# Attention in a decoder layer: the order of normalising, rope and query parts in a batch's third and fourth step

## The reference, cut to what matters

```
q = rope((ln(x) @ Wq.T).reshape(B, L, 32, 64));  k = rope((ln(x) @ Wk.T).reshape(B, L, 8, 64))
v = (ln(x) @ Wv.T).reshape(B, L, 8, 64)
attn = einsum(q, k) * 64**-0.5, causal;  p = softmax(attn);  out = einsum(p, v)
x = x + out.reshape(B, L, 2048) @ Wo.T
```

## Time and profile before

| | |
|---|---|
| median of 3 runs | 1603.34 us (1602.89 to 1606.78) |
| the profiled execution's own time | 1601.83 us |
| its span, first to last instruction | 1600.1 us |
| busy in the span: PE, DVE, ACT, POOL | 93%, 86%, 67%, 56% |

### The profile page before, as it was taken

How to read it: one execution, slowest core, us unless ns; L and a number is a source line. 1 busy time by engine, 2 the same in 40 slices (tenths; PEclk the granted TensorE clock), 3 DMA queues, 4 the chain that set the end, 5 groups by cost and what they waited for, 6 DMA issues and landing times. The chain is left out here.

```text
span 1600.1 us, 28647 instructions
## 1 busy us (share of the span) xinstructions
PE 1488.9 (93%) x8952; PEld 1306.1 (82%) x8952; DVE 1377.6 (86%) x3583; ACT 1066.6 (67%) x2464; POOL 902.1 (56%) x1024
## 2 busy tenths in 40 slices
PE   6799999999999999999999999779879999999998
PEld 4678878878878888888888887658779999999997
DVE  7799888989989898898898989668768889988996
ACT  3578778778777778778777777533146666666664
POOL 7668658667666666767667666268413443334432
PEclk9899999999999999999999999976589999999999
DMA  4000000000000000000000000042348788777761
GB/s 179 1 14 21 1 14 21 1 14 21 1 14 20 1 14 21 1 14 2 20 14 1 1 1 1 1 141 102 131 137 233 223 230 236 223 209 210 201 185 45
DMA packets 61925, 116.87 MB, mean 73 GB/s; under 512 B 22718, under 2 KB 22846, under 8 KB 61776
## 3 DMA queue, kind: packets, MB, share of 16 engines
q1 hardware_dynamic: 51328, 98.05, 19.0%
q0 software_dynamic: 10304, 16.94, 5.3%
q10 hardware_dynamic: 144, 0.07, 0.0%
HBM read 101.89 MB, written 20.51 MB: 76 GB/s over the span
## 5 line engine op out<-in xcount | busy, mean ns | idle before, releaser
L567 POOL TENSOR_SCALAR probs<-probs,row_inv 128x512 f32<-128x512 f32 (+3 forms) x512 | 296.2, 598 | 55.5 <-DVE row_inv L446 55.5
L330 ACT ACTIVATE probs<-probs,neg_max 128x512 f32<-128x512 f32 (+3 forms) x512 | 281.8, 552 | 12.2 <-DVE neg_max L439 6.7
L558 POOL TENSOR_TENSOR rot<-rot,sin 128x512 f32<-128x512 f32 (+1 forms) x96 | 124.3, 1295 | 251.2 <-DVE rot L458 248.7
L427 DVE TENSOR_TENSOR pt_lo<-bank,pt_hi 128x512 fp32r<-128x512 f32 (+1 forms) x384 | 217.8, 595 | 43.5 <-ACT pt_hi L323 43.5
L1285 POOL DMA_INDIRECT out<-ctx_raw,idx x46 | 93.8, 2038 | 266.4 <-ACT ctx_raw L1440 215.5
L439 DVE CUSTOM_DVE_ANT_0 probs<-bank,causal 128x512 f32<-128x512 f32 (+3 forms) x512 | 228.0, 481 | 7.3 <-PE bank L211 5.3
L223 PE MATMUL bank<-ident,probs 128*128 128x128 f32 x1280 | 184.1, 274 | 43.6 <-DVE pt_lo L427 43.2
L223 PEld LDWEIGHTS bank<-ident,probs 128*128 128x128 f32 x1280 | 150.8, 140 | 84.4 <-DVE pt_lo L427 51.7
L323 ACT ACTIVATE pt_hi<-bank 128x512 fp32r<-128x512 f32 (+1 forms) x384 | 186.5, 519 | 49.0 <-PE bank L223 43.6
L1367 PE MATMUL bank<-xt_hi,gu_hi 128*128 128x256 f32 x736 | 208.5, 283 | 3.5 <-issue 1.9
L1367 PE MATMUL bank<-xt_hi,gu_lo 128*128 128x256 f32 x736 | 206.6, 281 | 0.0
(11 more groups left out here) (204 smaller groups left out, 3980.6 us busy)
## 6 DMA issues: line engine op xcount, KB each, us to landing
gu_raw<-in_gate_up SPq DMA_DIRECT2D x92, 512.0 KB, 3.9
dn_raw<-in_down SPq DMA_DIRECT2D x92, 256.0 KB, 3.8
w_raw<-in_wqkv SPq DMA_DIRECT2D x8, 768.0 KB, 4.4
w_raw<-in_wo_rows SPq DMA_DIRECT2D x8, 512.0 KB, 3.5
h_rows<-ln_h SPq DMA_DIRECT2D x16, 256.0 KB, 2.1
out<-x_res SPq DMA_DIRECT2D x4, 1024.0 KB, 4.5
x_res<-in_x SPq DMA_DIRECT2D x3, 1024.0 KB, 11.2
ctx_raw<-in_ctx SPq DMA_DIRECT2D x2, 512.0 KB, 6.8
```

The source lines that it names most:

```text
L330: nc.scalar.activation(row, row, ACT.Exp, bias=neg_max[:, hb, i:i + 1], scale=-1.0, accum_out=row_sum[:, hb, i:i + 1]).then_inc(s["exp_don ...
L427: nc.vector.tensor_tensor(dst, src, hi.bitcast(F32), ALU.subtract).then_inc(sem_, 1)
L558: nc.gpsimd.tensor_tensor(rot[0:rows, :], rot[0:rows, :], sin[0:rows, :], ALU.mult).then_inc(s["rot_sin"], 1)
L567: nc.gpsimd.tensor_scalar(row, row, row_inv[:, hb, i:i + 1], 0.0, ALU.mult, ALU.add).then_inc(s["pnorm_done"], 1)
```

## The change

Three orders are altered; no instruction that computes is added or taken away.

- ACT, fourth step: the two copies of round 2 (`act_rope`) stand behind the four exponentials instead of in front of them. They still stand in front of `act_pt`.
- DVE, fourth step: `dve_q_lo` of round 2 stands behind the two `dve_pt` instead of in front of the reciprocal.
- POOL, third step: `pool_norm` stands in front of `pool_rope` instead of behind it. The wait of the weights' subtraction for `dve_q_lo` is dropped in the third step (it stays in the second).

```diff
--- before.py
+++ after.py
@@ -406,10 +406,12 @@
                 if h == 3 and next_batch:
                     act_v(act, m + 1, (b + 1) % 2)
-                if h and next_batch:
+                if h in (1, 2) and next_batch:
                     act_rope(act, m + 1, h - 1, (b + 1) % 2)
                 if more:
                     act_exp(act, n + 1, (r + c + 1) % 3)
+                if h == 3 and next_batch:
+                    act_rope(act, m + 1, 2, (b + 1) % 2)
                 if h == 0 and next_batch:
                     act_vt(act, m + 1, 3 * m + 4)
                 if d_here:
@@ -529,8 +531,8 @@
                 if h == 3 and next_batch:
                     dve_v(dve, m + 1, (b + 1) % 2)
-                if h >= 2 and next_batch:
-                    dve_q_lo(dve, m + 1, h - 1, (b + 1) % 2)
+                if h == 2 and next_batch:
+                    dve_q_lo(dve, m + 1, 1, (b + 1) % 2)
                 if h < 3 and next_batch and h != 2:
                     dve_rope_in(dve, m + 1, h, (b + 1) % 2)
                 if more:
@@ -538,6 +540,8 @@
                 if d_here:
                     dve_pt(dve, dn_, d % 2, 0)
                     dve_pt(dve, dn_, d % 2, 1)
+                if h == 3 and next_batch:
+                    dve_q_lo(dve, m + 1, 2, (b + 1) % 2)
                 if h == 2 and next_batch:
                     dve_rope_in(dve, m + 1, h, (b + 1) % 2)
                 if dh == 3 and d_last:
@@ -593,12 +597,14 @@
                 if h == 1 and next_batch:
                     pool_k_lo(pool, m + 1, (b + 1) % 2)
-                if h < 3 and next_batch:
+                if h < 2 and next_batch:
                     pool_rope(pool, m + 1, h, (b + 1) % 2)
                 if more:
                     pool_norm(pool, n + 1, (r + c + 1) % 3)
+                if h == 2 and next_batch:
+                    pool_rope(pool, m + 1, 2, (b + 1) % 2)
                 if (b, h) in W1_SLOTS and not (isinstance(g, int) and g == GROUPS - 1):
-                    if h < 3:
+                    if h == 1:
                         pool.wait_ge(s["q_lo_done"], 2 * m + 2 + h)
                     w1_lo(nc.gpsimd, pool, g + 1, W1_SLOTS[b, h])
```

## The result

The changed kernel takes 1623.48 us (median of 4 runs, 1619.96 to 1625.23), the kernel before 1605.06 (1602.89 to 1606.88) in the same comparison: a ratio of 1.0109, 95% interval 1.009 to 1.0128. It is slower: by 17.5 us by the ratio, by 18.4 between the medians. The profiled execution's span is 1618.2 us, 18.1 more than before.

What follows compares the result with a forecast made beforehand. The prediction took a ring through DVE, ACT and POOL, not PE, to bound the kernel. 17.7 us for the fourth steps plus 6.8 for third batches made 24.5, on 1601.83 giving 1626.3 us; range 1609 to 1633.

Steps and rivals of the forecast that it cites:

- Its ring: Chain through DVE, ACT and POOL from mask to mask: 22.02 us for three steps, 8.46 for the fourth, no slack.
- The gain of 0.97: Fourth step: `pt_lo` starts 0.97 us earlier, as the exponentials no longer wait for POOL's sum.
- the 1.54 of `dve_q_lo`: Fourth step, between `pt_lo` and `x_res`: two instructions at 1.42 us plus 0.12 in front add 1.54.
- +0.57: Net loss in us per batch in the fourth step: 1.54 added less 0.97 gained; 31 times makes 17.7.
- +0.23: Lower bound of the net loss per batch in us, if every spacing were the 0.60 of two `pt_lo`.
- PE's slack, not the kernel's price: Fourth step: PE's 1.03 us wait for the first `pt_lo` does not set the kernel's time.
- The meeting in third batches: Fourth step: POOL's weights' subtraction holds the second `dve_q_lo` instruction 0.97 us, in seven groups, 6.8 in all.
- the first rival: Third batches' fourth step: POOL's subtraction and `dve_q_lo` do not meet, so no 6.8 us; 1619.5 us; chance 0.33.
- The count: Number of fourth steps with the moved round 2, 31 of 32 batches, each charged 0.57 us.
- PE's new pause: Next batch's first step, at the transposes of unit 0: a pause of about 1.3 us opens on PE.
- the rope's lateness in third batches: Third step: POOL's rope up to half a microsecond late, covered by 1.3 us between sum and copies; no cost.

Runs made afterwards that it cites:

- the cut in PE's work: Kernel before, with 4 of the 6 output-projection matmuls left out in each fourth step: ratio 0.9998 to the kernel before, mask to mask 8.46 us.
- the 8 columns: Changed kernel with DVE's two query parts of round 2 cut to 8 of 512 columns: ratio 0.9902 to the kernel before, mask to mask 7.97 us.
- the second execution: Changed kernel run once more, unaltered: mask to mask 10.14 us in two of seven third batches, 9.02 in other fourth steps from the second on.
- POOL's part alone: Kernel before with only POOL's normalising moved ahead of the third step's rope and that step's wait dropped: ratio 1.0022 to the kernel before.

## Why the prediction was right

Its ring stands, with one correction: the prediction has PE only keeping the ring's pace, but from the end of its pause to the second step PE is on it, by some 0.16 us (above, behind the cut in PE's work). For the fourth step, where all that the change costs lies, this alters nothing. The first three steps were said to stay at 22.02 and measure 22.00; `pt_lo` was said to come 4.85 behind the mask (4.84), the next mask 9.03 (9.02). The gain of 0.97 measures 0.98, the 1.54 of `dve_q_lo` with its joints 1.53. The joints in front of, between and behind its two instructions measure 0.72, 0.70 and 0.72, not the 0.60 of two `pt_lo`, so +0.57 was the right choice over +0.23. The kernel before has the contrast at `o_f`, too: in the third step, where `o_f` stays in rows 0 to 63, the next instruction starts 0.59 behind it; in the fourth, where it moves rows, 0.72.

```profile
533.03 0.67 DVE L492 TENSOR_TENSOR o_f<-bank,v_and_o 64x512 f32<-64x512 f32 x1
533.62 0.67 DVE L502 TENSOR_TENSOR x_res<-bank,x_res 128x512 f32<-128x512 f32 x1
```

This agrees with the rule on instructions that start in another quadrant, which the prediction takes from the Trainium skill (VectorE: DVE Perf Modes, "Two Vector instructions with no wait between them"). "PE's slack, not the kernel's price" is shown for what PE does in front of its pause, by the cut that moved nothing, and the one-for-one price of DVE's place by the 8 columns.

Three terms were off in size.
- *The meeting in third batches*, 6.8 us: it measures 1.1 (one of seven), and 2.3 in the second execution. The place was right and the price nearly (1.14 instead of 0.97), but the two begin within hundredths of a microsecond and DVE mostly goes first. That was the first rival's condition, put at 0.33 against 0.50, and its 1619.5 lies nearest to the profiled execution's 1619.96. This term makes up nearly all that the forecast of 24.5 lies above the 18.1 measured; who goes first could not be read from the rows, and the range held either way.
- *The count*: 31 times 0.57. The first of the 31 gained and lost next to nothing (8.45 after, 8.40 before): `pt_lo` stood 6.36 behind the mask there before and 5.00 after, a gain of 1.36. 30 remain.
- *PE's new pause*: 1.3 us in one place was foretold. It is 0.40 and 0.64, the first in front of the output projection, whose PSUM bank waits for `x_res`; that wait was not foreseen.

That the rope's lateness in third batches is covered holds in the change and would not without ACT's part: alone, POOL's part loses 0.3 in each.

Why the change loses is then shown: with the query parts out of its way, its ACT order brings `pt_lo` forward by 0.98, its DVE order puts 1.53 behind `pt_lo`, on a ring in which these runs found no slack. That POOL's order neither costs nor brings anything in it is read from POOL's part alone; the other two parts were not run without it.

## What to carry to other kernels

A pause of the busiest engine shows which event is late, not that the engine is the bound: follow what the late event starts besides, and see whether that chain closes on itself. Here the fourth step's 8.46 us closed through DVE, ACT and POOL, of which the busiest is busy 86% of the span, PE 93%. Work that an engine does while it waits is free only where it waits: before an operation is moved behind a wait, ask what the engine would do in the wait instead; splitting the work in front (two exponentials, copies, two exponentials) kept both.

## What was not expected of the hardware

Which of two instructions that exclude each other had to wait was decided by hundredths of a microsecond: with starts at most 0.06 apart, DVE went first six times in seven in one execution and five in another. And a short DVE instruction cost less than its row: the reciprocal of 0.18 us delayed its successor by 0.10, while two `q_st` instructions of 0.69 took 1.42.
